# Row maxima of attention brought to the heads' rows by two DMA transfers per half of the queries, in place of identity matmuls and copies

## The reference, cut to what matters

```
x = x + conv(group_norm(x), ...)          # x: (8, 512, 32, 32) float32
# conv: per image, channels are split by a gate mask into two parts,
# each part goes through its own multi-head attention (8 heads of 64, 1024 tokens):
t = x.reshape(B, C, H * W).transpose(0, 2, 1)
q, k, v = jnp.split(t @ w_qkv + b_qkv, 3, axis=-1)
scores = jnp.einsum('bhnd,bhmd->bhnm', q, k) / jnp.sqrt(jnp.float32(hd))
attn = jax.nn.softmax(scores, axis=-1)
out = jnp.einsum('bhnm,bhmd->bhnd', attn, v)   # then @ w_o + b_o
# the first part's tokens pass a tanh scaling before and an arctanh scaling after
```

## Time and profile before

| | |
|---|---|
| median of 3 runs | 4022.97 us (4020.16 to 4023.03) |
| profiled execution, time | 4021.88 us |
| its span, first to last instruction | 4020.2 us |
| mean granted TensorE clock | 0.998 of full speed |
| busy: TensorE, VectorE, ScalarE, GpSimd | 3937.1, 2345.5, 1928.7, 2664.2 us |
| DMA, share of 16 engines | 21.2% in the SyncE queue |
| matmuls with the identity | 512, 44.7 us busy |
| ScalarE copies to `q_max` | 128, 69.0 us busy |

### The profile page before, as it was taken

The page is one execution under the profiler, slowest core; times in us unless marked ns, Lnnn a source line. Parts: engine busy times, 40 slices in busy tenths (PEclk is TensorE's granted clock), DMA queues, the critical chain, the costliest instruction groups (busy, mean ns, idle before and its releaser), DMA issues.

```text
span 4020.2 us, 57048 instructions
## 1 busy us (share of the span) xinstructions
PE 3937.1 (98%) x21664; PEld 2379.5 (59%) x21664; DVE 2345.5 (58%) x2553; ACT 1928.7 (48%) x3489; POOL 2664.2 (66%) x1303
## 2 busy tenths in 40 slices
PE   4999999999999999999999999999999999999998
PEld 3556566565655656556565665656556565565654
DVE  5464755647556475565746557465674656646455
ACT  4454534545345453555535545354553545535443
POOL 4584875838667486674857658675685756858468
PEclk9999999999999999999999999999999999999999
DMA  8212031121311213112141120411113121121101
GB/s 277 100 42 95 32 116 58 43 95 32 124 50 48 95 32 126 53 48 90 32 135 49 48 79 32 142 48 68 53 47 127 48 74 48 56 96 44 58 11 64
DMA packets 137548, 293.12 MB, mean 73 GB/s; under 512 B 16704, under 2 KB 28992, under 8 KB 127296
## 3 DMA queue, kind: packets, MB, share of 16 engines
q1 hardware_dynamic: 137280, 289.47, 21.2%
HBM read 239.09 MB, written 50.33 MB: 72 GB/s over the span
## 4 chain that ended last, share of the span: by engine, by line
PE 94%; DVE 2%; POOL 1%; DMA 1%; issue 1%; ACT 1%; SPq 0%; POOLq 0%; DVEq 0%; ACTq 0%
PE aux_ps L1310 32%; PE acc_ps L1422 23%; PE score_ps L1408 22%; PE aux_ps L1359 8%; PE score_ps L1310 4%; PE aux_ps L1432 3%; DVE mxp L1173 1%; PE aux_ps L1369 1%; POOL sums L673 1%; DMA w_split<-v_y 0%; DMA w_split<-w_o 0%; DMA xin<-in_x_dram 0%; PE aux_ps L1328 0%; PE aux_ps L1325 0%; POOL w_o L653 0%
## 5 line engine op out<-in xcount | busy, mean ns | idle before, releaser
L673 POOL TENSOR_TENSOR sums<-sums,probs 128x1024 f32<-128x1024 f32 x768 | 1835.4, 2390 | 736.9 <-ACT probs L850 682.6
L1173 DVE TENSOR_REDUCE mxp<-aux_ps 128x2 f32<-128x1024 f32 x1014 | 1241.7, 1225 | 1299.9 <-PE aux_ps L1359 1291.5
L850 ACT ACTIVATE probs<-score_ps 128x512 f32<-128x512 f32 x2048 | 1058.1, 602 | 658.7 <-PE score_ps L1408 648.0
L1422 PE MATMUL acc_ps<-probs,v_y 128*64 128x512 f32 x4096 | 991.9, 605 | 0.0
L1310 PE MATMUL aux_ps<-xs,w_qk 128*128 128x512 f32 x2976 | 804.7, 408 | 0.0
L1310 PEld LDWEIGHTS aux_ps<-xs,w_qk 128*128 128x128 f32 x2976 | 524.8, 188 | 374.3 <-issue 279.1
L673 POOL TENSOR_TENSOR sums<-probs 128x1024 f32<-128x1024 f32 x128 | 305.0, 2383 | 432.8 <-ACT probs L850 432.1
L1422 PEld LDWEIGHTS acc_ps<-probs,v_y 128*64 128x64 f32 x4096 | 248.2, 136 | 475.2 <-issue 245.2
L1359 PE MATMUL aux_ps<-k_hi,q_hi 64*128 64x512 f32 x2028 | 454.0, 443 | 18.7 <-DVE mxp L1173 16.1
L1235 DVE RECIPROCAL den<-den 128x256 f32<-128x256 f32 (+1 forms) x240 | 443.4, 1848 | 17.3 <-ACT den L861 17.3
L1408 PE MATMUL score_ps<-q_hi,k_hi 64*128 64x512 f32 x2048 | 407.9, 393 | 1.0 <-issue 1.0
(11 more groups left out here) (142 smaller groups left out, 3195.2 us busy)
## 6 DMA issues: line engine op xcount, KB each, us to landing
w_qk<-w_split SPq DMA_DIRECT2D x124, 512.0 KB, 4.2
xin<-in_x_dram SPq DMA_DIRECT2D x232, 256.0 KB, 3.3
w_o<-w_split SPq DMA_DIRECT2D x32, 1024.0 KB, 7.3
w_v<-w_split SPq DMA_DIRECT2D x30, 1024.0 KB, 5.9
v_y<-in_x_dram SPq DMA_DIRECT2D x72, 256.0 KB, 3.0
y<-v_y SPq DMA_DIRECT2D x64, 256.0 KB, 2.0
xin<-y SPq DMA_DIRECT2D x64, 256.0 KB, 2.9
out_dram<-v_y SPq DMA_DIRECT2D x64, 256.0 KB, 6.5
```

The lines of the kernel that those rows point to most:

```text
L673: pool.tensor_tensor(sums[h][:, :], a, probs[:, g % SLOTS_P, :], ALU.add).then_inc(c_sum[h].sem, 1)
L850: act.activation(probs[:, n % SLOTS_P, token_half(u % 2)], score_ps[:, u % SCORE_BANKS, :], ACT.Exp, scale=SCALE).then_inc(c_exp.sem, 1)
L1173: dve.tensor_reduce(mxp[:, :, n, h], ps, AX.X, ALU.max).then_inc(c_free["D"].sem, 1)
L1422: last = nc.tensor.matmul(acc_ps[head(j), :], v_y[:, m, head(2 * p + j)], probs[:, n % SLOTS_P, token_half(j)], start=(m == 0), stop=(m == ...
```

## The change

`mxw` becomes `[P, 2, 2, NT // 2]`: half of the queries, head, query tile. `combine` is called twice per pair, behind slot 11 for the first half of the queries and behind slot 15 for the second, with one instruction each. For each half, SyncE stores the 1,024 values of `mxw` to DRAM in the order of the rows, waits for that store, and loads the two rows of 512 into partitions 0 and 64 of `q_max`. The scores of a half wait for its load. The identity matmuls, their banks' use and ScalarE's copies are gone, and so are the identity matrix and its set-up.

```
+HALF_DONE = (11, 15)
+        max_dram = nc.dram_tensor("row_maxima", (2, 2, HALF), F32, kind="Internal").ap()
-        mxw = sb("mxw", [P, HD + NT], F32R)
+        mxw = sb("mxw", [P, 2, 2, NT // 2], F32R)
-        ident = sb("ident", [P, P], F32R)
...
+            def load_neg(i, t, p, h):
+                n = 0 if i is None else 4 * t + p
+                sp.wait_ge(c_mx.sem, c_mx.at(i, h + 1 if i is None else 2 * (n - 1) + h + 1))
+                if i is not None:
+                    sp.wait_ge(c_neg[h].sem, c_neg[h].at(i, 16 * (n - 1)))
+                sp.dma_start(max_dram[h].rearrange("j (n q) -> q (j n)", q=P),
+                             mxw[:, h, :, :].bitcast(F32).rearrange("p j n -> p (j n)")).then_inc(c_mst[h].sem, 16)
+                sp.wait_ge(c_mst[h].sem, c_mst[h].at(i, 16 if i is None else 16 * n))
+                last = TILES * t + 16 * (p - 2) + 8 * h + 8
+                if i is not None and (i or last > 0):
+                    sp.wait_ge(c_score.sem, c_score.at(i, 2 * last))
+                sp.dma_start(q_max[0:HD + 1:HD, p % 2, token_half(h)].bitcast(F32), max_dram[h]).then_inc(c_neg[h].sem, 16)
...
             for n, c in enumerate(SPLITS):
+                if n == len(SPLITS) - 1:
+                    load_neg(None, -1, PAIRS, 0)
...
                         load_wide(w_v, 1 - t, 4, c_wv)
+                    for h in range(2):
+                        load_neg(i, t, 1, h)
                     if t and followed(i):
                         load_chunks(i, 1, "operand", range(4), next_image)
...
                         load_chunks(i, 0, "operand", range(4))
+                    for h in range(2):
+                        load_neg(i, t, 2, h)
...
                         load_chunks(i, t, "operand", range(6, 8), next_image)
+                    for h in range(2):
+                        load_neg(i, t, 3, h)
...
                         load_qk(t, 5, 1)
+                        load_neg(i, t, PAIRS, 0)
...
                     if wanted(i, t, PAIRS):
+                        load_neg(i, t, PAIRS, 1)
                         load_qk(t, 6, 0)
...
-            def combine(i, t, p):
-                aux_read(dve, i, (t, "max", p, 15))
-                for j in range(2):
-                    dve.tensor_reduce(mxw[:, HD * j:HD * j + NT], mxp[:, j, :, :], AX.X, ALU.max,
-                                      negate=True).then_inc(c_mx.sem, 1)
+            def combine(i, t, p, h):
+                aux_read(dve, i, (t, "max", p, HALF_DONE[h]))
+                if i is not None:
+                    dve.wait_ge(c_mst[h].sem, c_mst[h].at(i, 16 * (4 * t + p - 1)))
+                dve.tensor_reduce(mxw[:, h, :, :], mxp[:, :, 4 * h:4 * h + 4, :], AX.X, ALU.max,
+                                  negate=True).then_inc(c_mx.sem, 1)
...
-                            if p:
-                                aux_read(pe, i, (t, "neg", p, 1))
...
+                        if m == 0:
+                            pe.wait_ge(c_neg[h].sem, c_neg[h].at(i, 16 * (4 * t + p)))
```

More of the change, by code:

```diff
@@ L179, in aux_tiles @@
                 out += [((t, what, pp, k), "D", (first, first + 1))]
-        return out + neg(p) + maxima(p + 1, 0)
+        return out + maxima(PAIRS + 1, 0)
     out = []
@@ L187, in aux_tiles @@
             out += [((t, "den", phase_at(b, DEN)), "A", (1,))]
-        if neg_pair(b) is not None and wanted(i, t, neg_pair(b)):
-            out += neg(neg_pair(b))
         if t == 0 and b in GATE_BATCH and followed(i):
@@ L334, in build @@
         c_mx = counted("max_made", 16, 2)
+        c_mst = [counted(f"max_stored{h}", 16 * 8, 16) for h in range(2)]
+        c_neg = [counted(f"max_rows_loaded{h}", 16 * 8, 16) for h in range(2)]
         c_score = counted("scores_made", NSC)
@@ L616, in _ @@
                 sp.wait_ge(c.sem, 17 + B * 128 - 16 * PAIRS + 16)
+            for c in (*c_mst, *c_neg):
+                sp.wait_ge(c.sem, 17 + B * 128 - 16)
             sp.wait_ge(c_wv.sem, 1 + B * 64 - 32)
@@ L620, in _ @@
         def _(pool):
[L621 removed]
             pool.memset(group_mean[:, :], 1.0 / GROUP).then_inc(s_const, 1)
             pool.memset(ones[:, :], 1.0).then_inc(s_const, 1)
[L624 removed]
             pool.memset(q_max[:, :, :].bitcast(F32), 0.0).then_inc(s_const, 1)
             pool.memset(first_row[:, :].bitcast(F32), 0.0).then_inc(s_const, 1)
[L627 to L634 removed]
+            pool.wait_ge(s_const, 4)
+            pool.memset(first_row[0:1, :].bitcast(F32), 1.0).then_inc(s_const, 1)
+            pool.wait_ge(s_const, 5)
+            pool.memset(first_row[HD:HD + 1, :].bitcast(F32), 1.0).then_inc(s_const, 1)
+            g3 = group_mean[:, :].rearrange("p (g c) -> p g c", c=GROUP)
+            pool.wait_ge(s_const, 6)
             pool.affine_select(out=g3, in_=g3, compare_op=ALU.is_ge, fill=0.0, base=0,
                                pattern=[[-GROUP, P // GROUP], [0, GROUP]], channel_multiplier=1).then_inc(s_const, 1)
[L638 removed]
+            pool.wait_ge(s_const, 7)
             pool.affine_select(out=g3, in_=g3, compare_op=ALU.is_ge, fill=0.0, base=GROUP - 1,
@@ L784, in qk_hi @@
                                bias=bias_q[:, tt, what, pp:pp + 1]).then_inc(c_hi.sem, 1)
-            def neg_rows(i, t, p):
-                for h in range(2):
-                    ps = aux_made(act, i, (t, "neg", p, h))
-                    act.activation(q_max[0:HD + 1, p % 2, token_half(h)], ps[0:HD + 1, :],
-                                   ACT.Copy).then_inc(c_free["A"].sem, 1)
             def split_hi(n):
@@ L890, in _ @@
                             den_copy(phase_at(b, DEN))
-                        if neg_pair(b) is not None and wanted(i, t, neg_pair(b)):
-                            neg_rows(i, t, neg_pair(b))
                         for j in HI_AT.get(b, ()):
@@ L1361, in max_slot @@
                 last.then_inc(c_aux.sem, 1)
-            def neg_rows(i, t, p):
-                pe.wait_ge(c_mx.sem, c_mx.at(i, 2 if t < 0 else 2 * (4 * t + p)))
-                for h in range(2):
-                    ps = bank_free(pe, i, (t, "neg", p, h))
-                    for n in range(4):
-                        last = nc.tensor.matmul(ps[0:HD + 1, n * P:(n + 1) * P], mxw[:, 4 * h + n:4 * h + n + HD + 1],
-                                                ident[:, :], start=True, stop=True)
-                    last.then_inc(c_aux.sem, 1)
             for g in GATES:
```

28 lines of the change are left out of this document (7 added, 21 removed).

## The result

The changed kernel takes 4039.81 us (median of 6 runs, 4035.13 to 4045.10) against 4021.82 us of the kernel before beside it: ratio 1.0045, 95% interval 1.0032 to 1.0058. It is slower by 18 us, where the forecast was 29 us faster. The profiled execution has a span of 4038.4 us, and the granted TensorE clock is 0.993 of full speed in the mean, 0.998 before.

A forecast was written before the change was run, and what follows sets the result against it. TensorE, busy 98% of the span, bounds the kernel. Removed blocks -36.8 and lead-in +6.4 give -30.4 us on 4021.88, 3991.5; with 1.1 for the runs' median, 3993 us, faster by 0.7%, range 3984 to 4012.

The forecast's parts named there:

- Removed (-36.8): In the images, the dropped matmul blocks save TensorE 36.8 us: 62 at 0.54, 2.0 of VectorE waits, 1.3 for the last.
- the earlier trace's 2.15: Products-to-block step in us, images 0 to 6, with a wait for VectorE's bank 1 read; forecast to become 1.87.
- The two transfers, in the images (0): In the images, store 3.5 us plus load 2.5 us, 6 us together, are hidden and cost TensorE zero.
- 17.1 us of cover: In each pair, time from the first half's maxima being complete to the scores that need them.
- the 9.4 us of cover at the image's end: Slack before ScalarE's first V copy, against about 4 us of SyncE delay; each microsecond beyond costs 7.
- Rival 1: A store of S us holds SyncE's result stores at image ends; whole gain gone at S = 13.3; slower, chance 0.08.
- The lead-in (+6.4): Before the images, transfers delay first scores from 94.01 to 102.0, 8.0 us, less 1.57 recovered: net 6.4 us lost.
- 99.6: Time in us near which the lead-in's store was to land, behind a split-weights store that lands after 14.4 us.
- can't overtake: Skill's ring-order rule as the prediction read it: a store just issued can't pass one in front; otherwise near 3984.
- 118 to 119.5: Forecast time of batch 1's x chunk, rather than 114.8; TensorE's 1.57 us wait behind VectorE there goes.
- VectorE (0): In batch 8p-3, the reduction moved to slot 11 delays some 0.2 us, is covered, and costs zero.
- The estimate of 38 us: Store time if the skill's 19 times for a rearranged-DMA transpose applied to a 2.0 us store; rival 1's worst.

The follow-up runs named there:

- lead_matmul: The changed kernel with the lead-in's row maxima turned by identity matmuls and ScalarE copies as before, the images keeping the transfers: 4000.12 us, ratio 0.9951.
- contig: The changed kernel with the DRAM copy laid out so the store writes 128 rows of 32 bytes and the load reads 4-byte elements: 4014.65 us, ratio 0.9981.

## Why the prediction was wrong

**Removed (-36.8).** Right in kind: the step is 1.87 us at all 62 places, and the earlier trace rows's 2.15 is gone. The size was some 20% too high (29.6 us with the last block), and 29% with the ends' loss below. The blocks' stretch gave 28.8 us, or 0.47 for each of 62, not 0.54. In the batch itself the shift fell by 0.53 (from 1266.41 - 1245.26 to 1268.28 - 1247.66); the rest came back in small steps before the next block. And at an image's end TensorE got the last block's time back and then waited 0.47 us for VectorE's o_t at L1249, which the block had covered: +3.4 in seven images. I had not looked for work that the block covered. The last block gave 0.8 us of 1.3.

**The two transfers, in the images (0).** The step that failed is "I take 3.5 us for the store". It takes 10.5 us in the median; I took as nearest a load of 4-byte elements, and it was no guide to a store whose elements lie side by side in DRAM. The load was sized well: the first one went out at 105.12, and the scores that waited for it started at 107.50. The covers were read rightly: TensorE never waited for the rows after the first, as 17.1 us of cover are more than 13, and the 9.4 us of cover at the image's end are near where losses begin (up to 9.0 us next to none in the kernel with its blocks; 8.8 us cost 0.7 in lead_matmul; from 9.7 us on all runs show some). Rival 1, with its break-even at S = 13.3, was the right mechanism. At S = 10.5 its formula gives 7 x (10.9 - 9.4) = 10.5 us; measured 15.9. It left out that W_o and xin are held too, and that VectorE's statistics wait for them: the begins show waits for ScalarE's V copy and for VectorE, and one of them the lower clock behind these.

**The lead-in (+6.4).** It cost 22.2 us. The store completed at 105.1, not 99.6. The 99.6 itself isn't what the rows add up to (84.20 + 14.4 = 98.6). That the store shares the landing of the one in front was right: the 1 MB store issued at 83.89 landed at 102.4, 18.5 us after its issue, and ours 2.7 us behind it. In contig, with rows of 32 bytes, it is 14.5 us, and 99.6 and 99.8. So the slow store seems also to have held up its neighbour, by 4 us. The section of the Trainium skill that the prediction names for the order adds that a later descriptor may finish its write before an earlier one, and that only the completion signal comes behind all earlier writes; "can't overtake" is said rightly of completion alone, and these two pairs agree. The scores started at 107.50, not 102.0. The second failure is larger: I let SyncE's queue recover, and put the first chunk of x at 118 to 119.5. But the second store stood in front of W_o and xin for another 12.1 us, and the chunk was there at 134.40. VectorE waited 12.56 us and TensorE 7.40, where I had the 1.57 us of the earlier trace rows vanish. I listed the second transfer in the queue and didn't add its landing. The clock is a third term: 2.5 us of the 22.2, for which the working had no step.

**VectorE (0).** Nothing from the moved reduction is seen in the ledger. But the 6.2 us in image 6 are a term for which the working had no step at all.

**The chances.** 0.08 for a slow store was too little for an operation of which no row existed, with the Trainium skill's rule on rearranged transposes speaking against it. The estimate of 38 us was itself far off, and it laid a factor against the hardware's transpose on the time of a plain store; 10.5 us were enough.

## What to carry to other kernels

An operation that no row of the trace shows is priced over its whole range, and each place that waits for it in order is worked through at the far end, with everything queued behind it, not only what is next. In a queue that is issued in order, put the wait for a store's completion behind the issues that don't need it; that was worth 19 us here. If a transpose goes through DRAM, let each partition write its own row and gather on the load. A wait of TensorE can cost more than its length: here the granted clock was at its lower level for 3.4 to 10.2 us behind some waits.

## What the runs showed that was not expected

A store whose 4-byte elements from different partitions lie side by side in DRAM takes 7 to 12 us to complete with little else in front of it, nearly whatever its size; with 64 bytes between them, or in rows of 16 or 32 bytes, it takes 2.4 to 2.7 us. A load that reads 4-byte elements from such rows was never seen to cost anything in the images. And four unused instructions at the start of the program took 7.6 us from a kernel, most likely by a phase of 0.1 to 0.2 us between VectorE and GpSimd.
